# Attention on a graph: queries in fp32, copied by ScalarE to fixed buffers, with a double-buffered stage in front

## What is computed

```python
q = (x @ Wq).reshape(n, H, HD)[src]
k = (x @ Wk).reshape(n, H, HD)[dst]
v_nodes = (x @ Wv).reshape(n, EH, HD)
ek = (edges @ Wek).reshape(-1, H, HD)
attn = jnp.einsum('ehd,ehd->eh', q, (k + ek) * scale)
attn = attn @ W_exp
```

## Time and profile before

| what | value |
|---|---|
| median of three runs without a profile | 6614.98 us |
| span of the profiled execution | 7688.3 us |
| node stage in it | 3946 to 4046 us |
| edge stage in it | 4047 to 5518 us |
| TensorE busy, weight loads busy | 51%, 40% |
| VectorE, ScalarE, GpSimd busy | 50%, 19%, 48% |
| mean granted TensorE clock | 0.653 of full speed |

### The profile page before, as it was taken

One profiled execution on the slowest core, in us unless ns is written; L12 is line 12 of the kernel. 1 busy time (PEld: TensorE's weight loads), 2 busy tenths in 40 slices (PEclk: granted clock), 3 DMA queues, 4 the chain that ended last, 5 costly groups with the idle time before them and its releaser, 6 DMA issues. The chain is left out here.

```text
span 7688.3 us, 103954 instructions
## 1 busy us (share of the span) xinstructions
PE 3918.9 (51%) x22797; PEld 3082.2 (40%) x22798; DVE 3809.0 (50%) x8547; ACT 1438.4 (19%) x3669; POOL 3692.0 (48%) x3791
## 2 busy tenths in 40 slices
PE   6746666556769523333343334333246635555556
PEld 4534445444546322222241222222135534444555
DVE  7845555555669633333353434333488833333333
ACT  6623333333320200000010000000023310101101
POOL 0054445444531166666616666666324345556552
PEclk9867777777789755555565555555569955555556
DMA  2066656656644211111116777776744411111111
GB/s 86 7 187 184 183 179 189 185 178 188 196 122 102 49 45 45 44 46 45 45 37 221 237 227 233 220 225 218 152 112 133 115 51 43 44 44 45 44 45 37
DMA packets 906173, 920.69 MB, mean 120 GB/s; under 512 B 329848, under 2 KB 744650, under 8 KB 905994
## 3 DMA queue, kind: packets, MB, share of 16 engines
q1 hardware_dynamic: 754906, 542.66, 25.6%
q0 software_dynamic: 138544, 371.96, 15.9%
q10 hardware_dynamic: 12672, 5.51, 0.3%
HBM read 678.28 MB, written 241.47 MB: 120 GB/s over the span
## 5 line engine op out<-in xcount | busy, mean ns | idle before, releaser
L953 POOL DMA_INDIRECT by_src<-edges_rows,edges_pos x832 | 860.0, 1034 | 903.9 <-issue 681.5
L1502 POOL DMA_INDIRECT edges_kv<-kv,edges_idx x896 | 915.3, 1021 | 700.5 <-issue 492.9
L2068 POOL DMA_INDIRECT sum_rows<-table,sum_idx x832 | 823.0, 989 | 649.9 <-DVE sum_msg L2112 311.1
L1258 POOL DMA_INDIRECT sum_rows<-table,sum_idx x832 | 787.2, 946 | 552.0 <-issue 246.4
L1335 PE MATMUL sum_p_sum<-sum_hot,sum_rows 128*128 128x128 f32 x1664 | 396.2, 422 | 830.4 <-DVE a_acc L1314 576.2
L1335 PEld LDWEIGHTS sum_p_sum<-sum_hot,sum_rows 128*128 128x128 f32 x1664 | 350.6, 312 | 876.2 <-DVE a_acc L1314 626.5
L2167 PE MATMUL sum_p_sum<-sum_hot,sum_msg 128*128 128x128 f32 x1664 | 425.2, 399 | 528.2 <-issue 459.2
L726 PE MATMUL edges_p_attr<-k_wekv,edges_attr 128*128 128x256 f32 x1664 | 575.9, 506 | 47.8 <-issue 30.9
L2167 PEld LDWEIGHTS sum_p_sum<-sum_hot,sum_msg 128*128 128x128 f32 x1664 | 359.8, 297 | 595.9 <-issue 594.4
L1612 PE MATMUL edges_p_q<-q_q,edges_src_hotT 128*128 x2688 | 418.1, 284 | 348.6 <-issue 282.7
L2127 DVE TENSOR_TENSOR a_acc<-a_acc,sum_p_sum 128x128 f32 x832 | 239.8, 288 | 694.1 <-DMA edges_attr<-in_attr128T 556.3
(11 more groups left out here) (376 smaller groups left out, 7648.6 us busy)
## 6 DMA issues: line engine op xcount, KB each, us to landing
edges_ekv<-by_src SPq DMA_DIRECT2D x112, 1024.0 KB
v<-edges_kv SPq DMA_DIRECT2D x112, 512.0 KB
sum_vv<-v SPq DMA_DIRECT2D x112, 512.0 KB, 3.9
edges_attr<-in_attr128T SPq DMA_DIRECT2D x104, 512.0 KB
edges_near<-h_in SPq DMA_DIRECT2D x832, 48.0 KB
sum_rows<-by_src SPq DMA_DIRECT2D x112, 264.0 KB, 3.0
edges_src_b<-rel SPq DMA_DIRECT2D x112, 256.0 KB
edges_dst_b<-dst SPq DMA_DIRECT2D x104, 256.0 KB
```

The source lines that it names most:

```text
L953: nc.gpsimd.indirect_dma_start(Dr.by_src0, bass.IndirectOffsetOnAxis(pos[:, q, j:j + 1], 0), rows[:, q % 2, j, :], None).then_inc(scattere ...
L1258: nc.gpsimd.indirect_dma_start(rows[:, q, j, :], None, Dr.table, bass.IndirectOffsetOnAxis(idx[:, q, j:j + 1], 0)).then_inc(fetched[q], 16)
L1502: nc.gpsimd.indirect_dma_start(kv[:, q, j, :], None, Dr.kv, bass.IndirectOffsetOnAxis(idx[:, q, j:j + 1], 0)).then_inc(fetched[q], 16)
L2068: nc.gpsimd.indirect_dma_start(rows[:, q, j, :], None, Dr.table, bass.IndirectOffsetOnAxis(idx[:, q, j:j + 1], 0)).then_inc(fetched[q], 16)
```

## The change

In the node stage `h` and `hT` get two buffers, and all loops are written out. TensorE issues the transposes of step i+1 ahead of the products of step i (`turn`, `project`), VectorE copies `hT` of step i+1 ahead of the queries of step i, and ScalarE normalises step i ahead of the kv copies of step i-1 (`keep`). The split goes: `K.q` holds fp32 and one VectorE copy per part fills it. The PSUM buffer `p_t` stays single.

In the edge stage `shot` becomes fp32. ScalarE loads the block numbers and copies the eight blocks of `K.q` to `near`, which has two buffers (`nearby`), in its queue behind `numbers(g+3)` and ahead of `scores(g-1)`. TensorE waits for them and makes one fp32 product per tile, with addresses fixed at build time.

```diff
 def nodes_before_attention(nc, K, Dr, s):
-    hs, hT, rest = s.sb("h", [P, R, D]), s.sb("hT", [P, R, D]), s.sb("rest", [P, 4, D])
+    hs, hT = s.sb("h", [P, 2, R, D]), s.sb("hT", [P, 2, R, D])
...
         @block.scalar
+            def keep(i):
                 for c, (r, n) in enumerate(parts):
-                    act.wait_ge(made, 2 * i + c + 3)
-                    act.wait_ge(stored[c], i * 16 + 16)
+                    act.wait_ge(made, 2 * i + c + 1)
+                    if i:
+                        act.wait_ge(stored[c], i * 16)
                     nc.scalar.copy(kv[:, c, 0:n, :].rearrange("p n f -> p (n f)"), p_kv[:, c].rearrange("p b n f -> p (b n f)")[:, 0:n * 2 * D]).then_inc(kv_kept, 1)
+            for i in range(NI):
+                if i > 1:
+                    act.wait_ge(turned, i - 1)
+                normed(nc, K, act, i, hs[:, i % 2], tick).then_inc(h_ready, 1)
+                if i:
+                    keep(i - 1)
+            keep(NI - 1)
...
         @block.tensor
+            def turn(i):
                 pe.wait_ge(h_ready, i + 1)
+                if i:
+                    pe.wait_ge(copied, i)
                 for r in range(R):
-                    tr = nc.tensor.transpose(p_t[:, r * P:(r + 1) * P], hs[:, r, :], K.ident[:])
+                    tr = nc.tensor.transpose(p_t[:, r * P:(r + 1) * P], hs[:, i % 2, r, :], K.ident[:])
                 tr.then_inc(turned, 1)
-                pe.wait_ge(copied, i + 2)
+            def project(i):
+                pe.wait_ge(copied, i + 1)
                 for c, (r, n) in enumerate(parts):
-                    pe.wait_ge(q_kept, (2 * i + c) * 5 + 5)
-                    pe.wait_ge(kv_kept, 2 * i + c + 1)
+                    if i:
+                        pe.wait_ge(q_kept, 2 * i + c - 1)
+                        pe.wait_ge(kv_kept, 2 * i + c - 1)
...
+            turn(0)
+            for i in range(NI):
+                if i < NI - 1:
+                    turn(i + 1)
+                project(i)
...
         @block.vector
-                    split3(nc, dve, p_q[:, c, 0:n, :], [K.q[:, bass.ds(i * R + r, n), k, :] for k in range(3)], rest[:, 0:n, :], q_kept, (2 * i + c) * 5 + 10, tick)
+                    nc.vector.tensor_copy(K.q[:, i * R + r:i * R + r + n, :], p_q[:, c, 0:n, :]).then_inc(q_kept, 1)
...
 def attention_edges(nc, K, Dr, s):
-    shot = s.sb("src_hotT", [P, 2, GE], BF16)
+    shot = s.sb("src_hotT", [P, 2, GE])
+    near = s.sb("q_near", [P, 2, G, D])
...
         @block.scalar
+            def nearby(g, h):
+                blk = load_values(nc, ACTE, K.srt_blk[0:1, bass.ds(g * G, G)], NB)
+                act.wait_ge(q_ready, 2 * g)
+                for j in range(G):
+                    ins = nc.scalar.copy(near[:, h, j, :], K.q[:, bass.ds(blk[j], 1), :].rearrange("p a d -> p (a d)"))
+                ins.then_inc(near_ready, 1)
+
             def group(g, q, stores, again, ahead):
                 h = q % 2
                 if ahead:
                     numbers(g + 3, (q + 3) % L, again)
+                nearby(g, h)
                 if stores is not None:
                     scores(g - 1, 1 - h)
                     logits(g - 1, 1 - h, stores)
...
         @block.tensor
             def queries(g, h):
-                blk = load_values(nc, PE, K.srt_blk[0:1, bass.ds(g * G, G)], NB)
                 pe.wait_ge(shot_ready, g + 1)
+                pe.wait_ge(near_ready, g + 1)
                 for c in range(2):
                     pe.wait_ge(prod_ready, 2 * g + c + 1)
                     pe.sem_inc(tick, 1)
                     for j in range(C * c, C * c + C):
-                        for k in range(3):
-                            mm = nc.tensor.matmul(p_q[:, h, c, j % C, :], shot[:, h, j * P:(j + 1) * P], K.q[:, bass.ds(blk[j], 1), k, :].rearrange("p a d -> p (a d)"),
-                                                  start=(k == 0), stop=(k == 2))
+                        mm = nc.tensor.matmul(p_q[:, h, c, j % C, :], shot[:, h, j * P:(j + 1) * P], near[:, h, j, :], start=True, stop=True)
                     mm.then_inc(q_ready, 1)
...
-                K.q = q.sb("q", [P, NB + 1, 3, D], BF16)
+                K.q = q.sb("q", [P, NB + 1, D])
```

More of the change, by code:

```diff
@@ L29 @@
 PE = mybir.EngineType.PE
+ACTE = mybir.EngineType.Activation
 P = 128
@@ L1388, in _ @@
         def _(act):
-            for c in range(2):
-                act.sem_inc(stored[c], 16)
-            act.sem_inc(kv_kept, 2)
-            with nc.scalar.Fori(0, NI) as i:
-                act.wait_ge(copied, i + 1)
-                normed(nc, K, act, i, hs, tick).then_inc(h_ready, 1)
+            def keep(i):
                 for c, (r, n) in enumerate(parts):
-                    act.wait_ge(made, 2 * i + c + 3)
-                    act.wait_ge(stored[c], i * 16 + 16)
+                    act.wait_ge(made, 2 * i + c + 1)
+                    if i:
+                        act.wait_ge(stored[c], i * 16)
@@ L1415, in _, with copy @@
                     mm.then_inc(made, 1)
+            turn(0)
[3 more added lines that the diff above has]
+                project(i)
         @block.vector
         def _(dve):
-            dve.sem_inc(copied, 1)
-            dve.sem_inc(q_kept, 10)
-            nc.vector.memset(K.q[:, NB:NB + 1, :, :], 0.0)
-            with nc.vector.Fori(0, NI) as i:
+            def copy(i):
                 dve.wait_ge(turned, i + 1)
-                dve.wait_ge(made, 2 * i + 2)
-                nc.vector.tensor_copy(hT[:].rearrange("p r d -> p (r d)"), p_t[:, 0:R * D]).then_inc(copied, 1)
+                if i > 1:
+                    dve.wait_ge(made, 2 * i - 2)
+                nc.vector.tensor_copy(hT[:, i % 2].rearrange("p r d -> p (r d)"), p_t[:, 0:R * D]).then_inc(copied, 1)
@@ L1426, in _ @@
+            nc.vector.memset(K.q[:, NB:NB + 1, :], 0.0)
+            copy(0)
+            for i in range(NI):
+                if i < NI - 1:
+                    copy(i + 1)
                 for c, (r, n) in enumerate(parts):
-                    dve.wait_ge(made, 2 * i + c + 3)
-                    dve.sem_inc(tick, 1)
-                    split3(nc, dve, p_q[:, c, 0:n, :], [K.q[:, bass.ds(i * R + r, n), k, :] for k in range(3)], rest[:, 0:n, :], q_kept, (2 * i + c) * 5 + 10, tick)
+                    dve.wait_ge(made, 2 * i + c + 1)
+                    nc.vector.tensor_copy(K.q[:, i * R + r:i * R + r + n, :], p_q[:, c, 0:n, :]).then_inc(q_kept, 1)
@@ L1433, in _ @@
             table = Dr.kv.rearrange("(b p) f -> p b f", p=P)
-            with nc.sync.Fori(0, NI) as i:
+            for i in range(NI):
                 for c, (r, n) in enumerate(parts):
-                    sp.wait_ge(kv_kept, 2 * i + c + 3)
-                    sp.sem_inc(tick, 1)
-                    nc.sync.dma_start(table[:, bass.ds(i * R + r, n), :], kv[:, c, 0:n, :]).then_inc(stored[c], 16)
+                    sp.wait_ge(kv_kept, 2 * i + c + 1)
+                    nc.sync.dma_start(table[:, i * R + r:i * R + r + n, :], kv[:, c, 0:n, :]).then_inc(stored[c], 16)
             for c in range(2):
-                sp.wait_ge(stored[c], 16 * NI + 16)
+                sp.wait_ge(stored[c], 16 * NI)
 def attention_edges(nc, K, Dr, s):
@@ L1461, in attention_edges @@
     l_stored = [s.sem("l_stored0"), s.sem("l_stored1")]
-    idx_ready, shot_ready, q_ready, kv_ready, prod_ready, score_ready, turned, scoreT_ready, mixed, logit_ready, tick = (
-        s.sem(n) for n in ("idx", "shot", "q", "kv", "prod", "score", "turned", "scoreT", "mixed", "logit", "tick"))
+    idx_ready, shot_ready, q_ready, kv_ready, prod_ready, score_ready, turned, scoreT_ready, mixed, logit_ready, tick, near_ready = (
+        s.sem(n) for n in ("idx", "shot", "q", "kv", "prod", "score", "turned", "scoreT", "mixed", "logit", "tick", "near"))
     with nc.Block() as block:
```

6 lines of the change are left out of this document (2 added, 4 removed).

## The result

The changed kernel takes 6634.3 us (median of 13 runs, 6625.0 to 6642.9), the kernel before in the same comparison 6620.9 us, a difference of 13.4 us. The ratio over all runs is 1.0024 with the interval 1.0017 to 1.0031, so it is slower by about 0.2%. 6599 us and "faster" were forecast.

A forecast was written before the change was run, and what follows sets the result against it. Outside the profile the edge stage was taken as bound by GpSimd's gathers, at about 1190 us. Node stage -16 us and edge stage 0 gave 6615 - 16 = 6599 us, range 6586 to 6640.

The forecast's parts named there:

- The 1073 us: Whole kernel before: profiled span 7688.3 us against median 6614.98 us; the excess was put down to being profiled.
- the 283 us: Edge stage before: the part of its 1471 us that is not gather time, counted among the profile's 1073 us.
- GpSimd-bound at 1190 us: Edge stage outside the profile: 112 groups of eight gathers at 10.6 us each set its length.
- The loop: Edge stage: one turn per group through transpose, idx copy, block-number load, ScalarE copies and products, 9.0 us against GpSimd's 10.6.
- The loop above GpSimd: Rival, edge stage: a turn above 10.6 us, for example 11.1, adds 56 us, giving 6655 us, slower; chance 0.22.
- the two signs named for being wrong: Edge stage, undisturbed stretches of the profile after: GpSimd waits for idx, or a turn is above 10.6 us.
- The edge stage at +0: Edge stage: the longer VectorE, ScalarE and TensorE work stays under GpSimd's 10.6 us per group, so costs 0 us.
- GpSimd is held longer: Rival, edge stage: the longer one-hot holds gathers for its extra 0.20 us, 22 us in all, giving 6621; chance 0.12.
- The node stage: Node stage: two buffers take hT's copy off the chain, steps of 11.95 us, 83.6 us against 99.7, gain 16.
- The upper end of the forecast: Node stage: TensorE's clock rises 1.75 us earlier, six steps give back 0.9 us each, gain 22 us.

The follow-up runs named there:

- f1_changed: The changed kernel itself, unedited, timed again beside the kernel before while register steps stalled: ratio 0.9979 (0.9953 to 1.0006).
- e7_slow_loop: The changed kernel with 24 more ScalarE copies of 16 columns per group, ahead of the eight query copies; stalled, 7546.7 us against 7511.7.
- g3_one_port: The changed kernel with its fp32 one-hot in two instructions into padded rows, one element at a time; without stalls 6567.4 us against 6622.2, ratio 0.9922.

## Why the prediction was wrong

**Stalls taken for the profile's.** The 1073 us between span and median were put down to the profile. They don't belong to it: the kernel before has a span of 6615.4 us beside a median of 6614.3, and on other occasions a median of 7488 to 7710 us. The use made of it, to leave the 283 us out of the edge stage, was harmless for that stage's bound. The rest, GpSimd-bound at 1190 us, was 1247 in truth, since the gathers among stalls are a little shorter (1021 against 1037 ns) and ramp-up, end and the 27 us of waits weren't counted.

**The loop: right.** Copies 0.20 us apart and 1.70 us for eight, as computed; products 3.4 to 3.75 us; a turn of 9.0 us forecast, 8.7 to 9.8 seen in `f1_changed` and 9.8 in `e7_slow_loop`. The errata's exposed 224 cycles (the Trainium skill, VectorE: DVE Perf Modes, § The TRN2 errata) would have made the eight copies an estimated 2.35 us; the trace has 1.70. The loop above GpSimd, at 0.22, didn't happen: of the two signs named for being wrong, GpSimd waits at one place near the end alone, and the loop's own turn stays under 10.6 us. Both looked at the loop, and the failure lay elsewhere.

**The edge stage at +0: the step that failed.** The one-hot's time was costed on VectorE, where it has slack, and not on GpSimd, which sets the stage. The rival "GpSimd is held longer" had the mechanism and nearly the price: 0.20 us more on 112 gathers, 22 us; it is 0.27 us more on some 100, 28 us. It got 0.12 because the one long gather in the earlier trace rows stood beside the add and "the 0.95 us gathers dominate". They do, and say nothing: what counts was in the mean of 1021 ns. Sorting the gathers of that trace by what runs beside them shows 112 beside the add alone, 0.50 us longer each, so a VectorE operation does hold gathers. And the bf16 one-hot holds them there too: 18 gathers, by 0.19 us on average, few, since among the stalls most gathers don't start beside it. One stands in the very stretch of the earlier trace rows, just ahead of the 1.97 us that were read:

```profile
4623.22 0.48 DVE L1570 TENSOR_SCALAR edges_src_hotT<-edges_src_b,k_node_col 128x1024 bf16<-128x1024 bf16 x1
4623.31 1.20 POOL L1502 DMA_INDIRECT edges_kv<-kv,edges_idx  x1 [0.30 <-issue]
4623.61 2.35 DVE L1581 TENSOR_TENSOR edges_kv<-edges_kv,edges_ekv 128x1024 f32<-128x1024 f32 x2
```

The gather starts 0.09 us behind the one-hot and ahead of the add, and takes 1.20 us; the 0.39 us that are left of the one-hot, less 0.12, and the 0.95 give 1.22. So the profile at hand did show the mechanism, and with it that a longer one-hot costs the gather what it is longer. How many gathers would meet it without stalls it didn't show. The rule that the prediction quoted (the Trainium skill, SBUF — State Buffer, § Who interferes with whom) holds here: `g3_one_port` takes the two-element form away and the extra goes from 48.5 to 0.1 us.

That 6634 lies within 13 us of that rival's 6621 is partly luck. In the spans the edge stage costs 12 us more than the rival's 22, the node stage gives 9 more than 16, and the weighted sums, which it left out, take 13.

**The node stage: right in kind, too small.** 16 us forecast (13 to 22), 24.6 measured.

A step of the changed kernel:

```profile
3458.99 0.80 ACT L1396 COPY nodes_kv<-nodes_p_kv 128x768 f32<-128x768 f32 x1 [0.95 <-PE nodes_p_kv L1426]
3459.68 2.80 ACT L514 ACTIVATE nodes_h<-k_x,k_shift,k_rstd 128x128 f32<-128x128 f32 x7
3462.54 1.75 PE L1414 MATMUL nodes_p_t<-k_ident,nodes_h 128*128 128x128 f32 x7 [3.58 <-ACT nodes_h L514]
3464.08 0.63 PE L1425 MATMUL nodes_p_q<-k_wqkv,nodes_hT 128*128 128x128 f32 x2
3464.51 1.06 PE L1426 MATMUL nodes_p_kv<-k_wqkv,nodes_hT 128*128 128x256 f32 x2
...
3465.70 0.60 PE L1426 MATMUL nodes_p_kv<-k_wqkv,nodes_hT 128*128 128x256 f32 x2
...
3469.61 0.80 ACT L1396 COPY nodes_kv<-nodes_p_kv 128x768 f32<-128x768 f32 x1 [0.95 <-PE nodes_p_kv L1426]
3470.31 2.03 ACT L514 ACTIVATE nodes_h<-k_x,k_shift,k_rstd 128x128 f32<-128x128 f32 x5
```

The chain is the one described: kv copy (3458.99), norm, transposes, products, kv copy (3469.61), norm. This step is 10.6 us where 11.95 was forecast. Its terms are norm 2.86, transposes until the first product 1.54, products until the last kv copy 5.53, that copy 0.70. The mis-sized term is the products, 5.53 instead of 6.65. A product of 256 columns (two records) takes 1.06 us at 3464.51 and 0.60 from 3465.70 on, so from the second tile of this step the clock is at its upper level (2.4 GHz). Counted from last kv copy to last kv copy, the five steps between the first products and the last take 12.1, 10.8, 10.8, 10.6 and 12.1 us; in the two of 12.1 the clock rises only in the fourth tile. In the kernel before, a step that I looked at has the upper level from within the fourth tile on (3468.66):

```profile
3467.38 1.06 PE L1414 MATMUL nodes_p_kv<-k_wqkv,nodes_hT 128*128 128x256 f32 x2
3468.23 0.63 PE L1413 MATMUL nodes_p_q<-k_wqkv,nodes_hT 128*128 128x128 f32 x2
3468.66 0.69 PE L1414 MATMUL nodes_p_kv<-k_wqkv,nodes_hT 128*128 128x256 f32 x2
3469.19 0.39 PE L1413 MATMUL nodes_p_q<-k_wqkv,nodes_hT 128*128 128x128 f32 x2
3469.41 0.60 PE L1414 MATMUL nodes_p_kv<-k_wqkv,nodes_hT 128*128 128x256 f32 x2
```

There TensorE waits 2.1 us between transposes and products; after, the products follow the transposes at once. The upper end of the forecast had this thought and gave it 0.9 us a step. It is 1.1 to 1.3 us in three of the five steps and nothing in the other two, and the first products end 1.2 us sooner and the last take 1.1 less than counted. So 78.1 us instead of 83.6; another 3.0 us lie in the kernel before, whose stage takes 102.7 us in the quiet trace and 99.7 in the earlier trace rows.

**An untouched stage.** Nothing was forecast for the weighted sums, and they are 13.2 us longer. TensorE does them at 0.79 of full speed in after and at 0.91 in before. The groups by line, before:

```profile
L1872 PE MATMUL sum_p_sum<-sum_wv,sum_hot 128*128 128x136 f32 x1792 | 292.9, 313 | 148.5 <-DVE sum_hot L1823 120.7 <-ACT sum_p_sum L1792 20.9 <-issue 6.9
```

After:

```profile
L1901 PE MATMUL sum_p_sum<-sum_wv,sum_hot 128*128 128x136 f32 x1792 | 332.3, 344 | 119.2 <-DVE sum_hot L1852 95.3 <-ACT sum_p_sum L1821 11.9 <-issue 10.7
```

The 17 traces of kernels with the new node stage have this stage at 477.7 to 487.8 us, the three with the old one at 473.8, 474.2 and 480.0. What ties the clock there to a change some stages ahead wasn't tried and stays open. By size it is as large as the whole difference of the medians, so a part of what went wrong has no shown cause: with the edge stage at +0 the span would have been 10.4 us shorter than before instead of some 24.

So, in profiled spans: -24.6 + 34.1 + 13.2 + 1.0 elsewhere = +23.7 us.

## What to carry to other kernels

When GpSimd issues the gathers that set a stage, cost every edit of a VectorE operation twice: on VectorE, and on the gathers that start beside it. A faster form that writes two elements at a time can be dearer than a slow one: twice the one-hot time on VectorE (0.75 to 1.47 us a group) took 65 us off the stage, 48 of them gather time beside the one-hot and 21 beside the add, whose share depends on where it falls. Before blaming the profile for idle time, measure the unchanged kernel again and compare its span with its own median.

## What the hardware showed that was not expected

- The add of two fp32 operands from SBUF (1.22 us) lengthens gathers that start while it runs, by what is left of it less about 0.12 us: up to 1.06 us each, 48 to 70 us a stage; the product with one operand in PSUM (0.68 us) and the reduction (1.22 us) by nothing. It is now the largest part of the extra time; it wasn't tried to write it otherwise.
- Register steps of 46 ns take up to 1.4 us in stretches, on several engines together, at some times and not at others, for every kernel: 870 to 1100 us of 7490 to 7710. Such times can turn the sign of a comparison: the one-hot one element at a time read 1.0002 to 1.0052 there and 0.9922 without.
- ScalarE copies of 16 columns start 0.11 us apart (24 in 2.63 us, each 0.20 long), those of 128 columns 0.20 (eight in 1.70 us, each 0.29 long).
